# A reordered ramp and turn in an attention and mixture-of-experts kernel: keep rows first, query products in quarters, two groups of plain fp32 work a turn

## The reference

```python
x = x + xattn(_layernorm(x), ctx, ctx, mask)      # x 16 x 112 x 256, ctx 16 x 375 x 256
x = x + ffn(_layernorm(x))

# xattn
q, k, v = heads(query @ Wq.T + bq), heads(key @ Wk.T + bk), heads(value @ Wv.T + bv)
scores = einsum('bhqd,bhkd->bhqk', q, k) / sqrt(16)
scores = where(mask == 0, -1e9, scores)
out = softmax(scores) @ v ; return out @ Wo.T + bo
# ffn
gate = softmax(flat @ router_w) ; top 2, their weights divided by their sum
y = sum over the two experts of weight * (silu(flat @ w1[e]) @ w2[e])
```

## Time and profile before

| | |
|---|---|
| Median of 3 runs | 480.66 us (478.79 to 482.40) |
| The profiled execution | 481.81 us, its span from first to last instruction 480.1 us |
| TensorE matmul / weight load busy | 416.9 us / 387.9 us |
| VectorE, ScalarE, GpSimd busy | 342.5, 277.1, 224.2 us |
| Transpose of maxima: of batch 0, 1, 15 | 55.8, 79.27, 274.1 us |
| Mean granted clock of TensorE | 0.93 of full |

### The profile page before, as it was taken

The page is one execution under the profiler, slowest core; times in us unless marked ns, Lnnn a source line. Parts: engine busy times, 40 slices in busy tenths (PEclk is TensorE's granted clock), DMA queues, the critical chain, the costliest instruction groups (busy, mean ns, idle before and its releaser), DMA issues.

```text
span 480.1 us, 10756 instructions
## 1 busy us (share of the span) xinstructions
PE 416.9 (87%) x4187; PEld 387.9 (81%) x4187; DVE 342.5 (71%) x698; ACT 277.1 (58%) x373; POOL 224.2 (47%) x253
## 2 busy tenths in 40 slices
PE   2766769999999999999999998688999999999810
PEld 1655659999899999999998987677999999999810
DVE  6854454887787888887878868866697766676545
ACT  3535443656666565566654553526778888888600
POOL 6533361322443222442321364846687788876420
PEclk9967987999999999999999999559999999999975
DMA  8799456688767777876643029933122322332168
GB/s 247 221 229 244 135 155 136 138 162 177 156 149 169 159 144 165 184 163 126 151 102 54 3 89 317 358 115 89 56 90 76 89 89 89 83 87 73 45 230 272
DMA packets 60291, 69.83 MB, mean 145 GB/s; under 512 B 19249, under 2 KB 55362, under 8 KB 60242
## 3 DMA queue, kind: packets, MB, share of 16 engines
q1 hardware_dynamic: 54002, 56.02, 47.3%
q0 software_dynamic: 4032, 11.02, 7.8%
q10 hardware_dynamic: 2208, 2.12, 1.3%
HBM read 35.29 MB, written 14.78 MB: 104 GB/s over the span
## 4 chain that ended last, share of the span: by engine, by line
PE 75%; DVE 8%; DMA 6%; issue 3%; ACT 3%; SPq 3%; POOL 1%; POOLq 0%; DVEq 0%; ACTq 0%
PE ps L1537 38%; PE ps L1598 12%; PE ps L1613 9%; PE ps L1627 9%; DMA x_rows_sb<-x_rows 2%; PE ps L1897 2%; PE ps L1640 1%; DMA y_back<-y_rows 1%; DVE neg_max L1103 1%; DMA y_rows<-y_out,slot_of_row 1%; DMA rows<-xn_rows,token_of_row 1%; SPq L450 1%; SPq L408 1%; DMA q_stack<-q_lo 1%; DMA q_stack<-max_rows 1%
## 5 line engine op out<-in xcount | busy, mean ns | idle before, releaser
L1103 DVE TENSOR_REDUCE neg_max<-ps 112x1 f32<-112x376 f32 x256 | 133.9, 546 | 49.0 <-PE ps L1598 44.6
L836 ACT ACTIVATE probs<-ps 125x1344 f32<-125x1344 f32 x64 | 82.8, 1293 | 49.3 <-PE ps L1613 42.2
L1598 PE MATMUL ps<-k_stack,q_stack 98*112 98x376 f32 x256 | 87.9, 378 | 11.8 <-DVE neg_max L1103 7.4
L604 POOL TENSOR_TENSOR k_lo<-k_f,k_hi 128x752 fp32r<-128x752 f32 x16 | 28.8, 1802 | 119.6 <-ACT k_hi L810 119.6
L1598 PEld LDWEIGHTS ps<-k_stack,q_stack 98*112 98x112 f32 x256 | 45.4, 179 | 23.8 <-DVE neg_max L1103 15.5
L766 POOL DMA_INDIRECT rows<-xn_rows,token_of_row x42 | 55.4, 1319 | 19.0 <-issue 12.2
L774 POOL DMA_INDIRECT y_rows<-y_out,slot_of_row x42 | 46.2, 1099 | 27.1 <-ACT y_out L1030 16.1
L1613 PE MATMUL ps<-q_stack,k_stack 100*125 100x224 f32 x384 | 53.7, 276 | 0.6 <-DMA q_stack<-max_rows 0.6
L1613 PEld LDWEIGHTS ps<-q_stack,k_stack 100*125 100x125 f32 x384 | 51.8, 192 | 1.6 <-DMA q_stack<-max_rows 0.8
L1537 PE MATMUL ps<-w_hi,h_hi 128*128 128x256 f32 x168 | 48.7, 290 | 1.6 <-issue 1.6
L1537 PE MATMUL ps<-flat_t_hi,w_hi 128*128 128x256 f32 x168 | 47.6, 283 | 1.3 <-DVE flat_t_lo L1424 1.3
(11 more groups left out here) (208 smaller groups left out, 1028.7 us busy)
## 6 DMA issues: line engine op xcount, KB each, us to landing
k_stack<-k_hi SPq DMA_DIRECT2D x64, 188.0 KB, 4.4
w_all<-w SPq DMA_DIRECT2D x2, 4096.0 KB, 18.2
k_stack<-k_lo SPq DMA_DIRECT2D x32, 188.0 KB, 5.4
ctx_raw<-ctx_t SPq DMA_DIRECT2D x32, 187.5 KB, 5.2
q_stack<-q_scratch SPq DMA_DIRECT2D x30, 168.0 KB
q_scratch<-q_hi SPq DMA_DIRECT2D x16, 224.0 KB, 3.0
y_back<-y_rows SPq DMA_DIRECT2D x14, 256.0 KB, 5.3
q_scratch<-q_lo SPq DMA_DIRECT2D x8, 224.0 KB, 3.0
```

The lines of the kernel that those rows point to most:

```text
L604: pool.tensor_tensor(kl[:, :, :], kf[:, :, :], kh[:, :, :].bitcast(F32), ALU.subtract)\
L836: act.activation(pf[j % 2][:, :, :], ps[0:CT, BK_ST:BK_ST + KT, 0:4 * S], ACT.Exp).then_inc(pf_ready, 1)
L1103: dve.tensor_reduce(neg_max[:, s:s + 1], ps[0:S, BK_MAX + s % 2, 0:CP], AX.X, ALU.max, negate=True).then_inc(max_read, 1)
L1598: pe.matmul(ps[0:S, BK_MAX + a, 0:CP], qs[b.ring][0:R_MAX, q, S * a:S * (a + 1)], ks[b.ring][0:R_MAX, q, :], start=True, stop=True).then_i ...
```

## The change

In the turn on TensorE, all four output quads of batch b now run in turn b: two of them behind the output transposes of batch b-1, in the middle, and two at the end, behind the transposes of the maxima and of the normalised rows. The other pieces are rearranged around that; on VectorE one maximum moves behind the first key tile; on ScalarE the context's high part goes before the keys', and `attn_high` behind exps 3; on GpSimd the context's low part goes before the keys'.

In the ramp, the keep rows' write to DRAM goes ahead of the rest of x, x comes in three loads, the loads of wo, bo and the router go behind the stacks of the second batch, `write_queries` of groups 2 and 3 move into SP's turns 0 and 1, and single waits for the writes replace one wait for all. The first context's low part moves from GpSimd to VectorE. Query groups 1 and 2 are cut into quarters (one tile, one half: three products) and put between pairs of heads; group 3 comes after the transpose of the first batch's maxima and the third batch's keys. A fourth home for a context lets `ctx_high` of batch 3 wait for the weights instead of the query writes. Buffers are laid out anew for that.

```diff
 def ctx_home(n):
-    return n if n < 2 else (0, 2, 1)[(n - 2) % 3]
+    return n if n < 2 or n == 3 else (0, 2, 1)[(n - 2) % 3]
...
@@ SP
                 if not early(b, 1):
+                    sp.wait_ge(q_written[b.n // GB % 2], queries_written(b.n // GB))
...
+                if b.n == RINGS - 1:
+                    sp.wait_ge(xt_done, NG)
+                    sp.wait_ge(ql_ready, NG)
...
                     stack_keys(b.after(2))
+                if b.n < 2:
+                    write_queries(b.n + 2)
...
-            load_rows(slice(GB, B), xr_rest_in)
             sp.wait_ge(keep_ready, 1)
             sp.dma_start(keep_scratch, keep_all[:, :]).then_inc(mask_written, 16)
+            load_rows(slice(GB, 2 * GB), xr_rest_in)
+            sp.wait_ge(mask_written, 16)
+            load_keep(0, slice(0, 2))
             load_ctx(second)
             load_weight(2, wv_t)
-            sp.wait_ge(mask_written, 16)
-            load_keep(0, slice(0, 2))
-            load_weight(3, wo_t)
...
+            sp.wait_ge(xr_rest_in, 16)
+            load_rows(slice(2 * GB, B), xr_rest_in)
...
-            load_keep(1, slice(2, B))
...
             first_stack(sp, 1, ql[0])
+            write_queries(0)
             load_ctx(first.after(3))
-            write_queries(0)
+            load_keep(1, slice(2, B))
             stack_keys(second)
-            sp.wait_ge(q_written[0], 96)
             sp.wait_ge(filled, 4)
             stack_queries(second)
+            load_weight(3, wo_t)
...
             write_queries(1)
-            write_queries(2)
             stack_max(first)
-            write_queries(3)
-            for p in range(2):
-                sp.wait_ge(q_written[p], 96 * NG // 2)
...
@@ GpSimd
             keep_rows()
-            ctx_low(first)
             mask_rows()
+            pool.wait_ge(kproj_done, 1)
             ctx_low(second)
             key_low(first)
             fill(range(1, 5))
             key_low(second)
+            pool.wait_ge(xt_done, 2)
+            fill(range(5, N_FILLS))
+            ctx_low(first.after(2))
             query_low(1)
-            ctx_low(first.after(2))
             query_low(2)
             query_low(3)
-            for p in range(2):
-                pool.wait_ge(q_written[p], 96 * NG // 2)
-            fill(range(5, N_FILLS))
...
             def turn(b):
+                if has(b.after(3)) and b.n:
+                    ctx_low(b.after(3))
                 if has(b.after(2)):
                     key_low(b.after(2))
-                if has(b.after(3)):
+                if b.n == 0:
                     ctx_low(b.after(3))
@@ ScalarE
                 elif early(b, 4):
-                    for p in range(2):
-                        act.wait_ge(q_written[p], 96 * NG // 2)
+                    act.wait_ge(wl_ready, 3)
...
-                if has(b.after(2)) and b.n:
-                    key_high(b.after(2))
                 if has(b.after(3)) and b.n:
                     ctx_high(b.after(3))
                 if has(before):
                     out_copy(before)
+                if has(b.after(2)) and b.n:
+                    key_high(b.after(2))
...
+                if has(b):
+                    exps(b, 3)
                 if has(before):
                     attn_high(before)
-                if has(b):
-                    exps(b, 3)
@@ VectorE
             normalise_first()
-            x_stats(1)
+            dve.wait_ge(ch_ready, 1)
+            dve.tensor_tensor(cl[0][:, :, :], c_raw[0][:, :, :], ch[0][:, :, :].bitcast(F32), ALU.subtract)\
+                .then_inc(cl_ready, 1)
             x_low(0)
             attn_weight_low(1)
-            roots(1)
...
             keys(first, 0)
+            attn_weight_low(2)
             keys(first, 1)
-            attn_weight_low(2)
+            x_stats(1)
             dve.wait_ge(const_set, 3)
             first_query_low()
+            roots(1)
...
-            maxima(first, range(0, 4))
+            maxima(first, range(0, 2))
+            x_low(2)
+            maxima(first, range(2, 4))
             x_stats(3)
             maxima(first, range(4, 6))
-            x_low(2)
             roots(3)
-            maxima(first, range(6, 12))
+            maxima(first, range(6, H))
+            max_rows(first)
             x_low(3)
...
-                    maxima(after, range(11, 14))
+                    maxima(after, range(11, 13))
...
-                    maxima(after, range(14, H))
+                    maxima(after, range(13, H))
@@ TensorE, turn
-                outputs(before, 2)
                 heads(0)
                 values(0)
-                heads(1, 2)
-                outputs(before, 3)
-                heads(3)
+                heads(1)
                 values(2)
-                heads(4, 5)
+                heads(2, 3)
                 scores(0)
-                heads(6)
+                heads(4)
+                values(1)
+                heads(5, 6)
+                scores(1)
+                heads(7, 8)
+                keys(0, 0)
+                heads(9, 10)
+                scores(2)
                 if has(before):
                     out_transpose(before)
-                heads(7)
-                values(1)
-                heads(8, 9)
-                scores(1)
-                heads(10)
                 outputs(b, 0)
+                outputs(b, 1)
                 heads(11)
-                keys(0, 0)
+                keys(0, 1)
                 heads(12)
-                scores(2)
+                scores(3)
                 heads(13)
-                keys(0, 1)
-                heads(14)
                 keys(1, 0)
-                heads(15)
+                heads(14, 15)
                 keys(1, 1)
-                scores(3)
                 if has(after):
                     max_transpose(after)
                 if has(before):
                     attn_transpose(before)
-                outputs(b, 1)
+                outputs(b, 2)
+                outputs(b, 3)
@@ TensorE, ramp
-            head_scores(first, range(0, 4))
-            project_queries(1)
-            head_scores(first, range(4, 6))
             x_transpose(2)
-            head_scores(first, range(6, 10))
-            project_queries(2)
-            x_transpose(3)
-            head_scores(first, range(10, 14))
-            project_queries(3)
-            head_scores(first, range(14, H))
-            max_transpose(first)
+            for n, part in enumerate(all_parts):
+                head_scores(first, range(2 * n, 2 * n + 2))
+                project_queries(1, (part,))
+            for n, part in enumerate(all_parts):
+                head_scores(first, range(8 + 2 * n, 8 + 2 * n + 2))
+                if n == 3:
+                    max_transpose(first)
+                project_queries(2, (part,))
+                if n == 2:
+                    x_transpose(3)
             for t in range(KD):
                 project_keys(first.after(2), t)
+            project_queries(3)
             pe.wait_ge(qh_ready, KD * NG)
@@ TensorE, behind the turns
-            quad_outputs(before, 2)
...
-            quad_outputs(before, 3)
```

78 lines of the change are left out of this document (45 added, 33 removed).

## The result

The changed kernel is slower: 492.44 us in the median (491.78 to 494.5, four runs) against 479.73 us for the kernel before on the same chip, a ratio of 1.025 (1.021 to 1.029). The forecast was 483 in a range of 473 to 491. The profiled execution has a span of 490.0 us against 480.1, so 9.9 us are to be found in its trace.

The account below looks back on a forecast made before the run. TensorE's own instructions were taken to set the steady turns' time at full clock. Profiled 481.8 us, +14.6 for the turns (12.3 + 2.8 - 0.5), -12.3 for the ramp, gave 484.1, or 483 on the median's scale; range 473 to 491.

Parts of the forecast that it names:

- the waits that the new order makes: Steady turn, part two: waits on exponentials and VectorE's maxima add 1.6 us, making the turn 14.8; twelve turns +12.3.
- Part one: Steady turn: four groups of plain fp32 work become two, cutting TensorE's own work about 0.5 us, from 13.75 to 13.25.
- The last two turns: Turns without keys: less stands between quads, and row statistics come ahead of the maxima; +1.4 us each, +2.8.
- The tail: After the turns: two output quads leave it and give back 0.5 us, since exponentials bound that stretch too.
- (a): Ramp, up to the first head: earlier keep-rows write and VectorE work moved later bring it 3 us sooner (0 to 4).
- (b): Ramp, first batch's maxima: query products in quarters between heads remove VectorE's idle time, 9 us less.
- (c): Ramp: last query group and its copies now stand between the first batch's maxima and turn 0; +4 us (3 to 7).
- (d): Turn 0: without the 3.01 us stop and most of the slow clock, about 14 us instead of 18.3; -4.3.
- TensorE is the bound and the groups pay: Rival for the steady turns: waits are hidden, a turn takes 13.25 us, total 461; chance 0.10.
- Only the exponentials bind: Rival for the turns: 14.2 us a turn and less in the last two, +7 instead of +14.6, total 475; chance 0.17.
- Little from the ramp: Rival for the ramp: thinly loaded TensorE stays at the lower clock, ramp gives -6, total 489; chance 0.18.
- The turn is longer still: Rival for the turns: 15.2 us because the transposed rows' copy follows the last exponentials, total 488; chance 0.10.

Follow-up runs that it names:

- three short-cut kernels: Changed kernel with maxima over every second column, with exponentials of half of each quad, and with both: 488.5, 486.8 and 476.4 us, one run each.
- turn-only kernel: Kernel before with the changed kernel's turn on all engines and the old ramp: 505.86 us, ratio 1.052.
- no_max_wait: Changed kernel with the two stacked rows of maxima sent a turn early as zeros from a constant tile: 491.01 us, ratio 1.020.
- ramp_only: Changed kernel with the old turn on TensorE, ScalarE, VectorE and GpSimd, so only the ramp, its buffers and transfers are new: 472.59 us, ratio 0.981.
- kernel with both engines short: Changed kernel with maxima over every second column and exponentials of only half of each quad: 476.4 us, one run.
- half_max: Changed kernel with each maximum reading only every second column of its score row: 488.5 us, one run.
- ramp_norm_wo: ramp_only with x's third group normalised before the second batch's key copy, and output-weight and router high parts before the last query group's copies: 472.21 us, ratio 0.980.

## Why the prediction was wrong

**The sum, term by term.** Forecast 481.8 + 14.6 - 12.3; the profiled executions differ by +22.5 (turns +16.7 and +5.8) - 10.85 - 1.7.

- *Twelve steady turns: +12.3, measured +16.7.* This is the first of two steps that failed, under "the waits that the new order makes". Of the 4.4 us, 1.4 is size: 14.88 us against 13.74 in an undisturbed turn is 1.14, where I had 1.0 to 1.05. (My own terms, 13.25 + 1.6, give 14.85 and 1.10; 0.9 of the 1.4 went in rounding.) The other 3.0 is a wait that I did not have and so put at nothing: quad 0 behind the transfer of the stacked maxima. I read what each quad owes to the quad before, and never asked what the first one waits for; the move brings it from 5.13 to 3.92 us behind the transpose, and the transfers that land after 3.0 to 4.6 us were in the trace of before. With the transfer out of the way all steady turns from the second on are equal. Between the profiled execution and its forecast, 491.8 and 484.1, lie 7.7 us: 4.4 here, 3.0 in the last two turns, 1.4 in the ramp, less 1.2 in the tail.
- *Inside the undisturbed turn* the 1.6 us of waits were 1.4, in other places. Quad 1 waits 0.27, as said (0.3), and shows its load. Quad 2 does not wait for exponentials: heads 9 and 10, 0.37 late by VectorE instead of 0.15, take that wait's place, and quad 3, which I had even, shows its load. Heads 14 and 15 wait 0.24 instead of 0.3, the transpose of the maxima 0.32 as said. That both engines share the loss is shown by the three short-cut kernels. *Part one* was too good: I gave 0.5 for fewer groups, with 0.08 for the step from transposes to quads; that step is 0.17. With both engines short the turn is 13.56 to 13.64, where I had 13.25. The two errors nearly cancel, so 14.8 for 14.88 proves less than it seems.
- *The last two turns: +2.8, measured +5.8.* This is the second step that failed, as large as the transfer's wait: I gave them 1.4 each without working them out. VectorE's statistics and additions now stand ahead of three maxima instead of two, and in turn 14 TensorE waits 1.78 us for them and loses its clock behind it. Moved away they leave turns of 16.2, in sum 2.4 us above the old ones and near the 2.8 that I gave.
- *The tail: -0.5, measured -1.7.* I don't explain it. In the turn-only kernel the same tail gave nothing (205.95), in no_max_wait it took 206.6, and with the old code it took 205.9 to 207.5 in five profiles.
- *The ramp: -12.3, measured -10.85*, by (a) -0.6 for -3, (b) -11.5 for -9, (c) +6.6 for +4, (d) -5.4 for -4.3. In (a) I watched the keep rows' and VectorE's chain; the head stood behind TensorE's transposes of the third group of x, these behind its normalising, and that behind a key copy on ScalarE. One swap gives 1.6 us of it back. (b) is right in its mechanism: the earlier trace rows had 9.2 us of idle time there, 1.3 are left with quarters (in ramp_only); that is 7.9 of the 11.5 us, and the rest I don't explain. (c) is at the upper end that I named; the last query group's copies and an output weight's low part stand between, and moving the latter alone changed nothing.

**The rivals.** That TensorE is the bound and the groups pay (13.25 us a turn) is nearest to what the kernel with both engines short does; with them at their length it is wrong by 1.6 us a turn. "Only the exponentials bind" (14.2) is not half_max, where the turn is 14.41. Two came nearest to the time, neither by its mechanism. Little from the ramp (489): the ramp gave most of what was forecast. "The turn is longer still" (488): the steady turns are near its 15.2, 15.1 in the mean, but for another reason: the copy of the transposed rows is not late anywhere (ScalarE is idle 12.7 us in eleven turns ahead of it). The SP queue's two moved writes cost nothing that I can see: the context's copy waited 1.04, 1.08 and 0.53 us in turns 1, 2 and 6 (not at all before), and steady turns without the transfer's wait are all alike from the second on.

**The signs I had named** held where they were about mechanism: quads no closer than 2.20, transposes 14.9 apart, two waits for exponentials a turn, no stop of 3 us in turn 0. Of the two signs of being wrong, quads closer than 2.2 us and maxima after 71, neither came: they did not cover the steps that failed. The range's upper end, 491, was set by rivals that each move one term. Three terms went the same way.

The Trainium skill (Perfetto Trace Analysis, Optimization Strategy) says to find the gaps on the engine one optimises for and the semaphore that ends each. The steady turns of before have no gaps, so there it names nothing; the work for this change was to ask which waits were covered, and by how much. The trace agrees with the rule on the kernel after: the table of waits names all three.

## What to carry to other kernels

Before moving an instruction forward, list every wait it has, transfers too, and read for each how long before its start the releaser came, over all repeats and not in one: a cover of half a microsecond over a transfer that lands up to 1.6 us late is all that kept the old turn steady. Before calling a spread scatter, look at what else moves in the late repeats. On an engine that is full, the order of work is itself what hides two other engines' latencies; a saving of 0.1 us a switch is worth nothing if the pieces that it joins were the spacing between dependent ones. A change in several parts is worth measuring in parts: here one part is worth 8.4 us (472.59 against 480.99, faster than both kernels), and the other lost more than that.

## What the runs showed of the hardware

A VectorE subtraction of two 128x512 tiles took 0.70 us at 6.62 us of the changed kernel, beside a GpSimd instruction on one tile (6.28 to 8.80), and 1.59 and (the row at 53.30 above) 2.18 us where a GpSimd subtraction of two tiles ran beside it:

```profile
6.62 0.70 DVE L1095 TENSOR_TENSOR attn_w_lo<-w_raw,attn_w_hi 128x512 fp32r<-128x512 f32 x1
...
14.78 1.59 DVE L1095 TENSOR_TENSOR attn_w_lo<-w_raw,attn_w_hi 128x512 fp32r<-128x512 f32 x1 [1.51 <-ACT attn_w_hi L805]
```

```profile
14.01 1.82 POOL L610 TENSOR_TENSOR ctx_lo<-ctx_raw,ctx_hi 128x752 fp32r<-128x752 f32 x1 [5.21 <-ACT ctx_hi L821]
...
52.83 2.11 POOL L643 TENSOR_TENSOR q_lo<-q_f,q_hi 128x896 fp32r<-128x896 f32 x1 [4.75 <-ACT q_hi L893]
```

Both slow ones end 0.54 us after GpSimd's end (15.83 and 16.37; 54.94 and 55.48), as if they had only begun then. In ramp_norm_wo, where the same instruction stands at 48.35 with GpSimd idle, it took 0.69. It also bears on a price of the prediction: the scaled means at 15.93 of the earlier trace rows, counted as 1.56 us of VectorE's work, ended at 17.49, just behind a GpSimd subtraction in the kernel before; in the changed kernel, with none beside it, the same instruction took 0.16.

```profile
15.35 2.12 POOL L595 TENSOR_TENSOR ctx_lo<-ctx_raw,ctx_hi 128x752 fp32r<-128x752 f32 x1 [2.53 <-ACT ctx_hi L803]
```

```profile
24.97 0.16 DVE L1169 SCALAR_TENSOR_TENSOR less_mean<-moments,rstd 112x4 f32<-112x4 f32 x1
```

No run was made for this alone.

A transfer of 7 KB landed 1.81 to 1.83 us after its issue in the steady turns of the changed kernel that had no 16 KB transfer of the instruction queue beside it, and 2.5 to 3.6 us after it in those that had one. And a step between kinds of work within one precision has its price too: 0.17 us from transposes to output quads.
